# Expert stages: both parts of x in one moving operand of 512 columns, sums outside TensorE

## The reference

```
layer 0: 32 experts of inner width 256, sigmoid gates, 6 of 32 kept per token,
         and a shared expert of width 512
layer 1: 8 experts of inner width 352, softmax gates, 2 of 8 kept per token,
         and a shared expert of width 704
out = sum over experts of gate[t, e] * (silu(x @ w_gate[e]) * (x @ w_up[e])) @ w_down[e]
      + the shared expert, which has no gate
```

## Time and profile before

| | |
|---|---|
| median of 3 runs | 1390.57 us |
| the profiled execution's own time | 1390.28 us |
| its span | 1388.5 us |
| TensorE busy | 1339.3 us (96%), 10611 matmuls |
| VectorE busy | 1098.7 us (79%) |
| ScalarE busy | 971.2 us (70%) |
| mean granted TensorE clock | 0.991 |
| gate/up matmuls (L1572) | 3 x 768 |
| down matmuls (L1558) | 3 x 192 |

### The profile page before, as it was taken

The page is one execution under the profiler, slowest core; times in us unless marked ns, Lnnn a source line. Parts: engine busy times, 40 slices in busy tenths (PEclk is TensorE's granted clock), DMA queues, the critical chain, the costliest instruction groups (busy, mean ns, idle before and its releaser), DMA issues. The chain is left out here.

```text
span 1388.5 us, 28308 instructions
## 1 busy us (share of the span) xinstructions
PE 1339.3 (96%) x10611; PEld 888.2 (64%) x10611; DVE 1098.7 (79%) x2195; ACT 971.2 (70%) x1892; POOL 156.3 (11%) x216
## 2 busy tenths in 40 slices
PE   3999999999999999999999999999999999999999
PEld 3544444444444444444458999999977864568998
DVE  5999989899999999997587766666667667887675
ACT  1599999999999999999284555555535622785543
POOL 4122222112222222020000000000000000000000
PEclk9999999999999999999999999999999999998999
DMA  7566566665656665446204755545437523204651
GB/s 188 125 141 142 116 167 159 165 164 129 135 111 142 142 136 113 113 74 86 91 1 181 284 191 189 186 182 181 182 116 323 243 113 130 69 1 136 175 188 39
DMA packets 75338, 199.51 MB, mean 144 GB/s; under 512 B 35512, under 2 KB 43616, under 8 KB 63040
## 3 DMA queue, kind: packets, MB, share of 16 engines
q1 hardware_dynamic: 75024, 197.69, 49.9%
q10 hardware_dynamic: 192, 0.20, 0.1%
HBM read 170.64 MB, written 23.80 MB: 140 GB/s over the span
## 5 line engine op out<-in xcount | busy, mean ns | idle before, releaser
L754 ACT ACTIVATE probs<-bank 128x512 f32<-128x512 f32 x1024 | 542.0, 619 | 50.0 <-PE bank L812 47.9
L672 DVE TENSOR_REDUCE pm<-bank 128x1 f32<-128x512 f32 x736 | 466.3, 683 | 47.0 <-PE bank L793 46.6
L812 PE MATMUL bank<-qst,kst 52*128 52x512 f32 (+1 forms) x1024 | 334.6, 435 | 6.9 <-DMA qst<-nscratch 6.2
L793 PE MATMUL bank<-kst,qst 48*128 48x512 f32 x904 | 314.3, 450 | 21.2 <-DMA qst<-qsplit 20.1
L824 PE MATMUL bank<-probs,vext 128*32 128x256 f32 (+3 forms) x4024 | 293.7, 392 | 0.7
L812 PEld LDWEIGHTS bank<-qst,kst 52*128 52x128 f32 (+1 forms) x1024 | 162.6, 186 | 195.0 <-DVE pm L672 93.0
L1572 PE MATMUL bank<-e_xhi,e_hi 128*128 128x256 f32 (+1 forms) x768 | 219.4, 286 | 0.0
L1572 PE MATMUL bank<-e_xlo,e_hi 128*128 128x256 f32 (+1 forms) x768 | 219.1, 285 | 0.0
L1572 PE MATMUL bank<-e_xhi,e_lo 128*128 128x256 f32 (+1 forms) x768 | 219.1, 285 | 0.0
L824 PEld LDWEIGHTS bank<-probs,vext 128*32 128x32 f32 x4024 | 92.3, 109 | 116.8 <-issue 102.9
L793 PEld LDWEIGHTS bank<-kst,qst 48*128 48x128 f32 x904 | 139.8, 187 | 30.5 <-DMA qst<-qsplit 20.1
(11 more groups left out here) (251 smaller groups left out, 1767.2 us busy)
## 6 DMA issues: line engine op xcount, KB each, us to landing
raw<-wall SPq DMA_DIRECT2D x43, 1536.0 KB, 6.6
kst<-kscratch SPq DMA_DIRECT2D x192, 128.0 KB, 4.5
kscratch<-ksplit SPq DMA_DIRECT2D x15, 1024.0 KB, 4.3
kraw<-ctx_rows SPq DMA_DIRECT2D x16, 512.0 KB, 6.1
vraw<-ctx_vt SPq DMA_DIRECT2D x16, 512.0 KB, 6.2
ctxT<-ctxT SPq DMA_DIRECT2D x8, 1024.0 KB, 9.5
nat<-ctx_chunks SPq DMA_DIRECT2D x6, 1024.0 KB, 19.5
weights<-wscratch SPq DMA_DIRECT2D x16, 256.0 KB, 3.8
```

The lines of the kernel that those rows point to most:

```text
L672: nc.vector.tensor_reduce(max_at(p, 1), bank[:, pre_bank(p), :], AX.X, ALU.max).then_inc(pre_reduced, 1)
L754: nc.scalar.activation(probs[:, (XST * k + n) % PR, :], bank[:, score_bank(XST * k + n), :], ACT.Exp, scale=XSCALE).then_inc(probs_ready, 1)
L793: ins = nc.tensor.matmul(bank[:, pre_bank(p), :], qst[64 * j:64 * j + KR, h, tt * P:tt * P + P], keys, start=True, stop=True)
L812: nc.tensor.matmul(bank[:, score_bank(s), :], kst[64 * j:64 * j + rows, h % 2, m * P:m * P + P], qst[64 * j:64 * j + rows, h, :], start=Tr ...
```

## The change

The high and low parts of x are laid side by side in one tile `xboth`, 512 columns. The high weights are multiplied with both at once, one matmul of 512 columns; the low weights with the high part of x, 256 columns, added to the first half of the same bank. So the first half of a bank holds high*high + low*high of the weights' parts, the second half holds high weights times the low part of x, and the two halves have to be added. Gate and up each fill a bank, two banks a unit, in three pairs that take turns.

ScalarE copies the second half of the gate bank to `silu` and of the up bank to a new tile `up`; VectorE adds the first halves to them; Silu then runs in place, and `acts` multiplies two tiles of SBUF. `gu_ready` is counted twice a unit, after gate and after up. The order in a unit is new: ScalarE cuts the weights four ahead between its two copies, VectorE its weights three ahead between its two adds. The activation's high and low parts are made one unit later (`act_high` and `act_rest` for the unit before, at the end of `step`). The loop of experts 0 runs over 12 experts in 2 turns instead of 4 in 6. The small gate tiles use banks 4 and 5 instead of 6 and 7.

```diff
-    xhi = at(parts_at + 14, "xhi", [P, DC, T], F32R)
-    xlo = at(parts_at + 18, "xlo", [P, DC, T], F32R)
+    xboth = at(parts_at + 14, "xboth", [P, DC, 2 * T], F32R)
+    xhi, xlo = xboth[:, :, 0:T], xboth[:, :, T:]
...
+    def pair(s, j):
+        return ((0, 1), (2, 3), (6, 7))[(U * s + j) % 3]
...
 # TensorE
-                if not (isinstance(n, int) and u < 4):
-                    pe.wait_ge(act_made, u - 3)
+                if not (isinstance(n, int) and u < 3):
+                    pe.wait_ge(act_made, u - 2)
                 for m in range(2):
+                    half = bank[0:r, pair(s, j)[m], :]
                     for d in range(DC):
                         c = (m * DC + d) * P
-                        for p, (w, xs) in enumerate(((hi[s % R][j], xhi), (hi[s % R][j], xlo), (lo[s % R][j], xhi))):
-                            ins = nc.tensor.matmul(bank[0:r, b, m * T:m * T + T], w[:, c:c + r], xs[:, d, :],
-                                                   start=d == 0 and p == 0, stop=d == DC - 1 and p == 2)
-                ins.then_inc(gu_ready, 1)
+                        nc.tensor.matmul(half, hi[s % R][j][:, c:c + r], xboth[:, d, :], start=d == 0, stop=d == DC - 1)
+                        ins = nc.tensor.matmul(half[:, 0:T], lo[s % R][j][:, c:c + r], xhi[:, d, :], start=False, stop=d == DC - 1,
+                                               skip_group_check=True)
+                    ins.then_inc(gu_ready, 1)
...
 # ScalarE
+            def act_high(n, s, j):
+                b, u, r = place(s, j), n * U + j, plan.rows(n, j)
                 act.wait_ge(act_made, u + 1)
                 if not (isinstance(n, int) and u < 4):
                     act.wait_ge(down_done, u - 3)
                 nc.scalar.copy(ahi[0:r, b, :], acts[0:r, b % 2, :]).then_inc(act_hi, 1)
+
+            def step(n, s, j):
+                gate, upper = [bank[0:r, x, T:] for x in pair(s, j)]
+                act.wait_ge(gu_ready, 2 * u + 1)
+                if not (isinstance(n, int) and u < 4):
+                    act.wait_ge(act_made, u - 3)
+                nc.scalar.copy(silu[0:r, b, :], gate).then_inc(act_step, 1)
                 if later(n, s, j, AHEAD):
                     cut_high(act, *later(n, s, j, AHEAD))
+                act.wait_ge(gu_ready, 2 * u + 2)
+                nc.scalar.copy(up[0:r, b, :], upper).then_inc(act_step, 1)
+                act.wait_ge(summed, 2 * u + 1)
+                nc.scalar.activation(silu[0:r, b, :], silu[0:r, b, :], ACT.Silu).then_inc(act_step, 1)
+                if later(n, s, j, -1):
+                    act_high(*later(n, s, j, -1))
...
 # VectorE
+            def act_rest(n, s, j):
+                b, u, r = place(s, j), n * U + j, plan.rows(n, j)
+                dve.wait_ge(act_hi, u + 1)
+                if not (isinstance(n, int) and u < 4):
+                    dve.wait_ge(down_done, u - 3)
+                nc.vector.tensor_tensor(alo[0:r, b, :], acts[0:r, b % 2, :], ahi[0:r, b, :].bitcast(F32),
+                                        ALU.subtract).then_inc(act_ready, 1)
...
-                dve.wait_ge(silu_ready, u + 1)
+                dve.wait_ge(act_step, 3 * u + 1)
+                nc.vector.tensor_tensor(silu[0:r, b, :], silu[0:r, b, :], gate, ALU.add).then_inc(summed, 1)
+                if later(n, s, j, AHEAD - 1) and not (isinstance(n, int) and u + AHEAD - 1 < DONE):
+                    cut_rest(dve, *later(n, s, j, AHEAD - 1))
+                dve.wait_ge(act_step, 3 * u + 2)
+                nc.vector.tensor_tensor(up[0:r, b, :], up[0:r, b, :], upper, ALU.add).then_inc(summed, 1)
+                dve.wait_ge(act_step, 3 * u + 3)
                 if gated:
...
-                nc.vector.tensor_tensor(acts[0:r, b % 2, :], silu[0:r, b, :], bank[0:r, b, T:2 * T], ALU.mult).then_inc(act_made, 1)
-                if later(n, s, j, AHEAD - 1) and not (isinstance(n, int) and u + AHEAD - 1 < DONE):
-                    cut_rest(dve, *later(n, s, j, AHEAD - 1))
-                dve.wait_ge(act_hi, u + 1)
-                if not (isinstance(n, int) and u < 4):
-                    dve.wait_ge(down_done, u - 3)
-                nc.vector.tensor_tensor(alo[0:r, b, :], acts[0:r, b % 2, :], ahi[0:r, b, :].bitcast(F32),
-                                        ALU.subtract).then_inc(act_ready, 1)
+                dve.wait_ge(summed, 2 * u + 2)
+                nc.vector.tensor_tensor(acts[0:r, b % 2, :], silu[0:r, b, :], up[0:r, b, :], ALU.mult).then_inc(act_made, 1)
+                if later(n, s, j, -1):
+                    act_rest(*later(n, s, j, -1))
...
             over_units(dve, step)
+            act_rest(N - 1, N - 1, plan.last - 1)
```

More of the change, by code:

```diff
@@ L1403, in __init__, with experts @@
         self.w_lo = g.sem(name + "_w_lo")
-def experts(g, k, name, E, choose, gate_w, gate_loaded, plan, cb, parts_at, rings, AHEAD, DONE, C_UNIT,
+def experts(g, k, name, E, choose, gate_w, gate_loaded, plan, cb, parts_at, up_at, rings, AHEAD, DONE, C_UNIT,
             portions, first_loads, later_loads, first_chunk=None, out=None):
@@ L1469, in over_units @@
             for j in range(U):
-                step(n, n % 4, j)
+                step(n, n, j)
         if E > 8:
-            with eng.Fori(1, E // 4 - 1) as i:
-                for s in range(2, 6):
+            with eng.Fori(0, (N - 10) // 12) as i:
+                for s in range(6, 18):
                     for j in range(U):
-                        step(i * 4 + s, s % 4, j)
+                        step(i * 12 + s, s, j)
         for n in range(N - 4, N):
             for j in range(units_in(n)):
-                step(n, n % 4, j)
+                step(n, n, j)
     def place(s, j):
         return (U * s + j) % 4
+    def pair(s, j):
+        return ((0, 1), (2, 3), (6, 7))[(U * s + j) % 3]
     def later(n, s, j, d):
@@ L1488, in later @@
             return None
-        return n + q, (s + q) % 4, jj
+        return n + q, s + q, jj
     def cut_high(act, n, s, j):
@@ L1578, in step @@
                     for a in range(TA):
-                        ins = nc.tensor.transpose(bank[0:E, 7, a * P:a * P + P], gates.c[:, a, :], g.ident[:, :])
-                    ins.then_inc(c_turned, 1)
+                        ins = nc.tensor.transpose(bank[0:E, 5, a * P:a * P + P], gates.c[:, a, :], g.ident[:, :])
+                    ins.then_inc(gate_step, 1)
                 if later(n, s, j, -DLAG) and later(n, s, j, 1):
@@ L1586, in _ @@
             over_units(pe, step)
-            first, second, third, fourth = [later(N - 1, (N - 1) % 4, plan.last - 1, -d) for d in range(DLAG, -1, -1)]
+            first, second, third, fourth = [later(N - 1, N - 1, plan.last - 1, -d) for d in range(DLAG, -1, -1)]
             down(*first, 0)
@@ L1614, in _ @@
             else:
-                act.wait_ge(z_ready, 1)
-                nc.scalar.activation(gates.s[:, :, :], bank[:, 6, 0:TA * E].rearrange("p (a e) -> p a e", a=TA), ACT.Exp,
+                act.wait_ge(gate_step, 1)
+                nc.scalar.activation(gates.s[:, :, :], bank[:, 4, 0:TA * E].rearrange("p (a e) -> p a e", a=TA), ACT.Exp,
                                      scale=-1.0).then_inc(gate_exp, 1)
-            def step(n, s, j):
+            def act_high(n, s, j):
                 b, u, r = place(s, j), n * U + j, plan.rows(n, j)
-                act.wait_ge(gu_ready, u + 1)
-                if not (isinstance(n, int) and u < 4):
-                    act.wait_ge(act_made, u - 3)
-                nc.scalar.activation(silu[0:r, b, :], bank[0:r, b, 0:T], ACT.Silu).then_inc(silu_ready, 1)
                 act.wait_ge(act_made, u + 1)
@@ L1637, in _ @@
             over_units(act, step)
+            act_high(N - 1, N - 1, plan.last - 1)
             if out is None:
@@ L1712, in step @@
                 gated = [share for share in plan.shares(n, j) if not (isinstance(share[2], int) and share[2] < 2)]
-                dve.wait_ge(silu_ready, u + 1)
+                gate, upper = [bank[0:r, x, 0:T] for x in pair(s, j)]
+                dve.wait_ge(act_step, 3 * u + 1)
[5 more added lines that the diff above has]
+                dve.wait_ge(act_step, 3 * u + 3)
                 if gated:
```

26 lines of the change are left out of this document (13 added, 13 removed).

## The result

The changed kernel takes 1411.0 us (median of 4 runs, 1406.5 to 1415.3), the kernel before 1390.7 (1388.0 to 1391.6): ratio 1.0148, 95% interval 1.0117 to 1.0178. Slower, by 1.5%; forecast were 1408 us and a range of 1397 to 1418. The profiled execution took 1412.1 us, its span 1410.4. A second profile of the same kernel gave 1407.7 us, span 1405.9.

What follows compares the result with a forecast made beforehand. TensorE's columns were taken to bound both expert stages. First stage -1.8 us and second +19.1 gave +17.3 on the profiled 1390.3 us, or 1408 us against a median of 1390.6; 80% range 1397 to 1418.

Steps and rivals of the forecast that it cites:

- Part 1: TensorE gate/up: fewer, wider matmuls save 0.06 us a unit; bounds no gain and 0.31 us a unit.
- Rival B: TensorE: a pair costs only streaming, 0.320 us, saving 0.31 us a first-stage unit; total 1391 us; chance 0.04.
- Part 2: Added copies and adds: ScalarE 2.6 us, VectorE 3.5 us a unit, both below 4.20, hidden in first stage.
- its own slack: First stage: a late raw load has room, 6.6 us to landing in a period of 8.4 for two units.
- Part 3: Second stage: moved cut and later activation parts close a ring over 22 down products, costing 18.5 us.
- the ring: Second stage: down product releases cut, upper copy, Silu, product, low part, next down product; period 5.06 us against 4.20.
- the ungated rounds: Second stage: three rounds of the ring without weighting, forecast at 4.64 us each.
- the two weightings: Second stage: five rounds with two experts in a unit, weighting 0.89 instead of 0.46, 5.49 us each.
- Rival C: Second stage: ring doesn't bind if the chain from cut to low part takes under 2.8 us; 1388 us; chance 0.06.
- Part 4: Stage ends and starts: first stage start +0.9 and +0.2 us, end +1.2; second stage end +1.0.
- Rival D: First stage: VectorE or hand-overs bind too, 4.4 us a unit, +13.6 us, 1426 us; chance 0.04.
- rival E: Second stage: granted clock falls as TensorE idles, 8.4 us a unit at half clock, +71 us, 1479; chance 0.02.

Runs made afterwards that it cites:

- experiment 5: Kernel before plus only the pairs of 512- and 256-column matmuls in two banks; no copies or sums, order as before: 1384.1 us, ratio 0.9965.
- experiment 4: Changed kernel's whole arithmetic with all of the order of the kernel before, no parts put off: 1390.2 us, ratio 1.0002.
- experiment 1: Changed kernel with ScalarE's weight cut moved from between its two copies to the end of the unit: 1390.5 us, ratio 1.0001.
- experiment 3: Changed kernel with the activation's high and low parts made in their own unit again, cut left between the copies: 1397.7 us.
- Experiments 1 and 2: The second: changed kernel with ScalarE's cut behind Silu, ahead of the previous unit's high part: 1389.3 us; with more runs 1388.9 us, ratio 0.9993.
- Experiment 6: Pairs of matmuls with the changed order (cut ahead of Silu, parts a unit later), without copies and sums: 1403.8 us.

## Why the prediction was right, by its steps

**Part 1 (the pairs), right.** -0.06 us a unit forecast; 4.20 instead of 4.26 in the first stage, and experiment 5 has -3.8 and -2.0 us for -4.1 and -1.7. Neither bound (0 and 0.31) came near. Rival B is out.

**Part 2 (the added work is hidden), right in the sum, wrong in one reason.** The first stage has no wait of TensorE in its middle, and experiment 4 shows copies and sums free within a unit (4.20 us in both stages). But I gave the raw load "its own slack". ScalarE's waits for it in the first stage, 742 to 1030 us of the changed kernel:
```profile
ACT e_hi L1501 <- DMA raw<-wall: 38.6, 25, 4.2
```
It was 4.1 us, 3 times, before. The cut stands earlier in its unit, while the load can only be sent off when VectorE is done with the buffer. With the cut at the end of the unit (experiment 1) they are 5.6 us, 5 times: it is the cut's earlier place that asks for the load too soon. It cost TensorE nothing, since the cut is four units ahead, and not since the load had slack; experiment 3 shows what such a wait does where VectorE has nothing to make up for it.

**Part 3 (the ring), right.** 22 rounds, the number forecast. Down products of the changed kernel start 5.06 to 5.11 us apart with one share (forecast 5.06), 5.55 to 5.57 with two (5.49, five of them), 4.79 to 4.85 without weighting (4.64, three). From the first down product's start, 1278.13, to the 23rd, 1391.71, are 113.6 us, where the kernel before has 93.6 (1277.20 to 1370.78): +20.0 against +18.5. What I had too small are the ungated rounds by 0.2 each and the two weightings by 0.07 each, 0.9 us together; the rest is up to 0.05 in the other rounds and one of 5.24. TensorE's waits in these rounds add to 15.6 us, where I had named 18 to 20 as the sign: of the 0.89 us that a round of 5.09 loses, 0.61 to 0.64 count as idle, 0.16 hide in the last gate/up matmul, which lasts 0.28 where its pace is 0.12, and 0.11 in the first matmul after the wait.

That the stage came out at +19.9 for +19.1 is partly luck. Ahead of its first down product it took 13.24 us for 14.24 before, 1.0 less, where the forecast has 0.06 a unit. In experiment 5 it was 0.8 less, so most of it is the pairs, in a stretch that starts at a granted clock of 0.50; what a pair costs there I hadn't asked.

One link of the ring was named wrongly: not Silu but VectorE's upper sum carries the ring behind the upper copy (1305.99, 1306.39, 1306.73 for the weighting). Copy, Silu and weighting take 0.31 + 0.40 in the forecast, copy, sum and weighting 0.40 + 0.34 in the profile, so the sum came out the same. Where no weighting stands between, the product waits for the whole upper sum, 0.55 us from start to start, and that is the 0.2 of the ungated rounds:
```profile
1286.40 0.42 DVE L1746 TENSOR_TENSOR e_up<-e_up,bank 128x256 f32<-128x256 f32 x1 [1.53 <-ACT e_up L1643]
1286.95 0.43 DVE L1757 TENSOR_TENSOR e_acts<-e_silu,e_up 128x256 f32<-128x256 f32 x1
```

Rival C (the ring doesn't bind) said that it would take a chain under 2.8 us: it is 3.8 us (1304.18 to 1308.00), as forecast. Experiments 1 and 2 are rival C made true, at 120.5 and 120.3 us.

**Part 4 (ends and starts), right in sign and size.** End of the second stage, from the first down matmul behind the last gate/up group to the last one: 6.20 us (1400.59 to 1406.79) for 5.24 before (1379.68 to 1384.92), +1.0 as forecast. End of the first: 1.64 idle for 0.65, +1.0 for +1.2. The start is right in sum only: gate/up 3 waits 0.93 us for product 0, where I had 0.2, and the first down product 0.41 us for its low part, where I had 0.9. All that the first stage has over experiment 5 is 290.59 - 288.14 = 2.45 us, forecast 2.3. In the experiments with the ring open this costs 3.4 us (the first down product waits 1.3 to 1.4 us there), which is why the whole change, without its ring, is at 0.9993 and the pairs alone at 0.9965. Experiment 6, with the parts put off but no copies and sums, has 288.25, so it is the sum of two halves that, free in the middle, is paid where a stage begins and ends.

Rival D (the hand-overs bind in the first stage too) did not come true, but was nearer than its 0.04 says: with the parts in their own unit, VectorE takes 4.22 to 4.24 us on average for TensorE's 4.20 (experiment 3). Of rival E: the granted clock is 1.00 from 1270 to 1407 us, with idle times of 0.4 to 1.1 us in 22 rounds. What I called idle times of 1.0 and 1.8 us around 1029 us in the kernel before are distances from start to start; idle are 0.65 and 1.44 of them. And its +71 us is not quite what its terms give: 22 rounds at 8.4 for 5.10 are +73.

## What to carry to other kernels

Where an engine waits for a buffer to come free, ask not how long it waits, but what stands behind the waiting instruction in its order, and whether any of it leads back to the thing waited for within one period. 62 us of such waits were free in one order, 57 us cost 20 in another, and moving one instruction by two places took all of it back. Add up the ring link by link from start to start; here that gave 5.06 us for a measured 5.09, when busy shares of two thirds and half said that there was room. And a lag put in to take a hand-over out of an engine's unit (0.47 us in each here) is worth its own look: it shortens that unit and lengthens the ring.

## What the runs showed that I had not expected

- In experiment 3 VectorE needs 4.12 us in one unit and more in the next, 4.22 to 4.24 on average for a period of 4.20. A single unit read off the timeline looked as if it had room. What comes late isn't made up for, and the bill comes at the loop's turn and at the end of the stage (+9 us, 5.8 of them in the last two waits).
- Weighting to product takes 0.55 and 0.65 us in turn in the loop of the first stage, 0.45 where units are written out; in a ring that runs over it, this comes back in 48 units. The mechanism stays open.
- From a down product's last matmul to the start of the cut that waited for it, 0.43 us in the changed kernel and 0.51 in experiment 6, for the same wait of the same instruction. Not pursued.
